# Sequence half of a two-stage kernel: decay exponents from 32-row tiles, mask in fp32r, operands and a normalising moved, new order

## The reference

```python
# block 0 (spectral): fft2 over H, W; amplitude times two sigmoid gates (C x C products); ifft2;
# 3x3 convolution; swish; plus x; layer norm over C.  The change doesn't touch it.
# block 1 (sequence): every image row of 128 positions is a sequence of length 128
u  = layernorm(z)
zg, xBC, dt = split(u @ in_proj_w.T)            # 256, 384, 8 columns
xBC = silu(causal_conv(xBC, 4 taps) + conv_b)   # x: 8 heads x 32, B: 64, C: 64
dt  = softplus(dt + dt_bias);  A = -exp(A_log)
# per head: h = h * exp(dt*A) + dt*x (outer) B;  y = h . C
y   = ssm_scan(x, dt, A, B, C) + D * x
y   = rmsnorm(y * silu(zg)) * ssm_norm_w @ out_proj_w.T
z   = z + linear_ff(y)
out = z + fc2(gelu(fc1(layernorm(z))))
```

## Time and profile before

| | |
|---|---|
| runs | 4972.34 us median of 3 (4968.33 to 4972.8) |
| profiled execution | 4973.1 us, span 4971.3 us, mean granted PE clock 0.983 |
| PE busy | 4777.4 us (96%) |
| DVE, ACT, POOL busy | 3626.1, 3136.8, 1884.9 us |
| first half (spectral) | up to about 2115 us |
| sequence half | outputs from 2220.5 us on, one per step of 21.71 us |

### The profile page before, as it was taken

One profiled execution on the slowest core, in us unless ns is written; L12 is line 12 of the kernel. 1 busy time (PEld: TensorE's weight loads), 2 busy tenths in 40 slices (PEclk: granted clock), 3 DMA queues, 4 the chain that ended last, 5 costly groups with the idle time before them and its releaser, 6 DMA issues.

```text
span 4971.3 us, 93964 instructions
## 1 busy us (share of the span) xinstructions
PE 4777.4 (96%) x31687; PEld 3555.1 (72%) x31687; DVE 3626.1 (73%) x9341; ACT 3136.8 (63%) x4388; POOL 1884.9 (38%) x2150
## 2 busy tenths in 40 slices
PE   7999999999999999969999999999999999999998
PEld 4888669875988498736766666666667666666766
DVE  4346542655166615659999999999999999999997
ACT  4211421133112411159999999999999999999997
POOL 0011000110011001135566556656655665566564
PEclk9999999999999999979999999999999999999999
DMA  2012201230023001211111111111111111111110
GB/s 78 1 50 70 85 1 35 70 100 0 20 70 99 17 5 62 68 38 37 36 36 36 36 38 36 36 36 36 36 36 38 36 36 36 36 38 36 36 36 24
DMA packets 216359, 205.38 MB, mean 41 GB/s; under 512 B 15904, under 2 KB 150688, under 8 KB 216224
## 3 DMA queue, kind: packets, MB, share of 16 engines
q1 hardware_dynamic: 216224, 203.58, 13.1%
HBM read 136.41 MB, written 67.11 MB: 41 GB/s over the span
## 4 chain that ended last, share of the span: by engine, by line
PE 30%; ACT 23%; issue 3%; DVE 0%; ACTq 0%; POOL 0%; POOLq 0%; DVEq 0%
PE g_ps L935 6%; PE g_ps L931 5%; PE g_ps L874 4%; ACT g_acc L1041 3%; ACT L1101 3%; ACT L1135 3%; PE g_ps L919 3%; ACT g_tap L1046 3%; PE g_ps L903 3%; ACT g_emat L1078 2%; PE g_ps L920 2%; PE g_ps L965 2%; ACT L1098 2%; ACT g_gl L1093 2%; ACT g_bmat L1054 2%
## 5 line engine op out<-in xcount | busy, mean ns | idle before, releaser
L1186 DVE SCALAR_TENSOR_TENSOR g_acc<-g_ps,g_conv_w,g_acc 128x504 f32<-128x504 f32 (+2 forms) x896 | 651.6, 727 | 11.6 <-ACT g_tap L1046 11.6
L1243 DVE TENSOR_TENSOR g_mmat<-g_emat,g_ps 128x1024 f32<-128x1024 f32 x512 | 616.5, 1204 | 1.5 <-PE g_ps L892 0.8
L381 ACT ACTIVATE f_conv_v<-f_ps,f_bias 128x512 f32<-128x512 f32 x128 | 87.9, 687 | 782.3 <-PE f_ps L213 782.3
L1078 ACT ACTIVATE g_emat<-g_ps 128x1024 f32<-128x1024 f32 x512 | 494.4, 1017 | 44.3 <-PE g_ps L920 44.3
L919 PE MATMUL g_ps<-g_rz,g_l 128*128 128x512 f32 x1024 | 481.6, 532 | 27.7 <-ACT g_emat L1078 25.1
L211 PE MATMUL f_ps<-f_s_hi,f_wf_hi 128*128 128x512 f32 x1152 | 468.4, 407 | 2.3 <-DVE f_s_lo L398 2.3
L213 PE MATMUL f_ps<-f_s_hi,f_wf_lo 128*128 128x512 f32 x1152 | 457.9, 397 | 0.0
L212 PE MATMUL f_ps<-f_s_lo,f_wf_hi 128*128 128x512 f32 x1152 | 457.1, 397 | 0.0
L768 POOL TENSOR_TENSOR g_sqs<-g_sq 128x256 f32<-128x256 f32 x256 | 186.7, 729 | 660.6 <-ACT g_sq L1083 660.6
L920 PE MATMUL g_ps<-g_mask_b,g_ident_b 128*128 128x512 bf16 x1024 | 400.2, 391 | 0.0
L540 POOL TENSOR_SCALAR f_rstd<-f_mv 128x4 f32<-128x4 f32 x128 | 40.9, 320 | 839.4 <-DVE f_mv L414 839.4
(11 more groups left out here) (178 smaller groups left out, 12118.7 us busy)
## 6 DMA issues: line engine op xcount, KB each, us to landing
f_xt<-in_x_cols SPq DMA_DIRECT2D x128, 256.0 KB, 2.9
f_xres<-in_x SPq DMA_DIRECT2D x128, 256.0 KB, 2.7
z<-f_zout SPq DMA_DIRECT2D x128, 256.0 KB, 2.1
g_zin<-z SPq DMA_DIRECT2D x128, 256.0 KB, 2.7
g_zres<-z SPq DMA_DIRECT2D x128, 256.0 KB, 2.7
out<-g_outb SPq DMA_DIRECT2D x128, 256.0 KB, 2.0
f_wf_raw<-in_w_f SPq DMA_DIRECT2D x1, 576.0 KB, 5.1
g_wx<-in_in_proj_t SPq DMA_DIRECT2D x1, 192.0 KB, 2.5
```

The costliest lines, as they stand in the source:

```text
L1078: act.activation(emat[:, g, :].rearrange("p (b n) -> p b n", b=2), ps[:, D_BANK[g]:D_BANK[g] + 2, :], ACT.Exp).then_inc(e_a[g], 1)
L1186: dve.scalar_tensor_tensor(out=acc[:, j, :, k:], in0=four(ps[:, bank, :])[:, :, 0:P - k], scalar=conv_w[:, j, 3 - k:4 - k], in1=acc[:, j, ...
L1243: dve.tensor_tensor(mmat[:, g, :].rearrange("p (h n) -> p h n", h=HEADS), emat[:, g, :].rearrange("p (h n) -> p h n", h=HEADS), ps[:, CB, ...
```

## The change

Only the sequence half is changed.

- `decays`: the left operand is one [128, 128] tile in place of [128, 4, 128], laid out so that 32 partitions hold everything for one group and four heads (both parts of the sums on either side). For each half of the heads there is one matmul on 32 rows (`tile_position`), the two halves on neighbouring row groups into two banks; after both, two matmuls over the full array add the mask, which is now fp32r like its identity.
- The order of (group, head) in dt, dta, dtx and in the bias and A is permuted to fit (`blocks`); dt's bias is spread once before the loop.
- The left operand comes from one ACT pass over q (`left`), and the rows for `right` from another (`right_rows`); DVE's `right` then covers 128 partitions. POOL's `left` and the two constant passes of ACT go.
- The second norm is on POOL (`norm_h`, two passes of [128, 512]), DVE's `norm` goes.
- Other PSUM banks, other `held` waits, and a new order in every `body` except SP's: cross and all four decays of a quad are now in one step, ACT has four table loads per step (Silu, exponential and logarithm, Silu, Gelu).

```diff
+def blocks(t):
+    return t.rearrange("p (a b c h) -> p a b c h", a=2, b=2, c=2)
...
-        UT, HT, F1 = 0, 2, 4
-        X_BANK, BC_BANK, Z_BANK = (5, 2), 6, (0, 5)
-        CB, XT_BANK, D_BANK, Y_BANK = 4, (3, 5), (0, 2, 0, 2), (1, 3)
-        SS, OUT, F2 = 1, 4, 4
+        UT, HT, F1 = 4, 4, 3
+        X_BANK, BC_BANK, Z_BANK = (3, 2), 5, (2, 6)
+        CB, XT_BANK, D_BANK, Y_BANK = 0, (6, 1), (2, 0, 4, 4), (1, 6)
+        SS, OUT, F2 = 5, 6, 3
...
-            def left(x):
-                pool.wait_ge(q_d, x.n + 1)
-                held(pool.wait_ge, sqs_p[0], x.n, QUADS)
-                pool.tensor_tensor(l4[64:P], q[64:P, :].bitcast(FP).unsqueeze(1).to_broadcast([64, 4, P]),
-                                   ind_g[64:P, :].unsqueeze(2).to_broadcast([64, 4, P]), ALU.mult).then_inc(l4_p, 1)
+            def norm_h(x):
+                pool.tensor_tensor(hc[:, :, :], z2[:, :, :], mv2[:, :, 0:1].to_broadcast([P, 4, P]),
+                                   ALU.subtract).then_inc(hc_p, 1)
+                pool.wait_ge(r2_p, x.n + 1)
+                pool.wait_ge(hc_p, x.n + 1)
+                pool.tensor_tensor(hn[:, :, :], hc[:, :, :], r2[:, :].unsqueeze(2).to_broadcast([P, 4, P]),
+                                   ALU.mult).then_inc(hn_p, 1)
...
             def decays(x, g):
                 pe.wait_ge(rz_d, x.n + 1)
-                pe.wait_ge(l4_p, x.n + 1)
-                if g == 0:
-                    pe.wait_ge(e_a[2], x.n + 1)
-                if g == 1:
-                    pe.wait_ge(e_a[3], x.n + 1)
+                pe.wait_ge(l4_a, x.n + 1)
                 if g == 2:
                     held(pe.wait_ge, rsv_d, x.n, QUADS)
                 if g == 3:
-                    held(pe.wait_ge, conv_d[1], x.n * 2 + 4, 2 * QUADS)
+                    pe.wait_ge(e_a[2], x.n + 1)
                 for half in range(2):
-                    dst = four(ps[:, D_BANK[g] + half, :])
-                    pe.matmul(dst, l4[:, g, :], rz[:, 4 * half:4 * half + 4, :], start=True, stop=False)
-                    mm = pe.matmul(dst, ident_b[:, :], mask_b[:, :].unsqueeze(1).to_broadcast([P, 4, P]),
-                                   start=False, stop=True)
+                    rows, first = slice(64 * (g // 2) + 32 * half, 64 * (g // 2) + 32 * half + 32), 4 * (g % 2)
+                    pe.matmul(four(ps[:, D_BANK[g] + half, :]), l4[rows, :], rz[rows, first:first + 4, :],
+                              start=True, stop=False, tile_position=(rows.start, 0))
+                for half in range(2):
+                    mm = pe.matmul(four(ps[:, D_BANK[g] + half, :]), ident_r[:, :],
+                                   mask_r[:, :].unsqueeze(1).to_broadcast([P, 4, P]), start=False, stop=True)
                 mm.then_inc(d_mm[g], 1)
...
+            def right_rows(x):
+                act.wait_ge(q_d, x.n + 1)
+                act.activation(qr[:, :], q[:, :].bitcast(FP), ACT.Identity, bias=sides[:, 1:2], scale=sides[:, 0:1]).then_inc(qr_a, 1)
+
+            def left(x):
+                act.wait_ge(q_d, x.n + 1)
+                act.activation(l4[:, :], q[:, :].bitcast(FP), ACT.Identity, bias=sides[:, 0:1], scale=sides[:, 2:3]).then_inc(l4_a, 1)
...
             def right(x):
-                dve.wait_ge(q_d, x.n + 1)
-                dve.tensor_tensor(rz[0:64], q[0:64, :].bitcast(FP).unsqueeze(1).to_broadcast([64, HEADS, P]),
-                                  p_indh[0:64, :].unsqueeze(2).to_broadcast([64, HEADS, P]), ALU.mult).then_inc(rz_d, 1)
+                dve.wait_ge(qr_a, x.n + 1)
+                dve.tensor_tensor(rz[:, :, :], qr[:, :].unsqueeze(1).to_broadcast([P, HEADS, P]),
+                                  p_indh.unsqueeze(2).to_broadcast([P, HEADS, P]), ALU.mult).then_inc(rz_d, 1)
```

More of the change, by code:

```diff
@@ L976, in body @@
                     project_bc(a_)
+                    project_z(a_, 1)
                 if b:
-                    cross(b)
-                    decays(b, 0)
-                    decays(b, 1)
-                if a_:
-                    project_z(a_, 1)
-                    project_z(a_, 0)
+                    mix(b, 0)
+                if c:
+                    turn_h(c)
                 if b:
                     mix(b, 2)
+                if c:
+                    ffn1(c)
+                if b:
                     mix(b, 3)
+                    mix(b, 1)
                 if a_:
                     cumulate(a_)
-                if b:
-                    mix(b, 0)
+                    project_z(a_, 0)
                 if p:
@@ L993, in body @@
                 if c:
[L994 removed]
+                    ffn2(c)
+                if b:
+                    project_out(b)
+                    sums(b)
+                if a_:
+                    decays(a_, 1)
+                if p:
+                    project_dt(p)
+                if a_:
+                    decays(a_, 2)
+                    decays(a_, 0)
+                    cross(a_)
+                    turn_x(a_, 0)
+                    decays(a_, 3)
+                if p:
+                    project_x(p, 0)
                 if a_:
                     turn_x(a_, 1)
[L997 to L1002 removed]
                 if p:
                     project_x(p, 1)
[L1005 to L1015 removed]
             pipeline(pe, QUADS, body)
@@ L1136, in body @@
+                    left(a_)
                     silu_c(a_)
+                    silu_b(a_)
+                    silu_x(a_, 1)
+                    act.preload_act_table_set("natural_log_exp_and_others")
+                    exps(a_, 1)
+                    exps(a_, 2)
+                    exps(a_, 0)
                 if p:
                     absolute(p)
+                    exp_dt(p)
+                if a_:
+                    exps(a_, 3)
+                if p:
+                    second_tap(p, 0)
+                    tap(p, 0)
+                    log_dt(p)
+                    second_tap(p, 1)
+                    act.preload_act_table(ACT.Silu)
+                    silu_z(p, 1)
+                    tap(p, 1)
@@ L1140, in _ @@
+                if b:
+                    affine_h(b)
+                if p:
+                    tap(p, 2)
+                if b:
+                    act.preload_act_table(ACT.Gelu)
+                    gelu(b)
             pipeline(act, QUADS, body)
@@ L1346, in body @@
                 if a_:
-                    scale_x(a_, 0)
-                if p:
-                    taps(p, 1, 2)
-                    add_bias(p)
+                    right(a_)
             pipeline(dve, QUADS, body)
```

230 lines of the change are left out of this document (86 added, 144 removed).

## The result

The changed kernel took 5061.4 us (median of 4 runs, 5056.7 to 5071.5) against 4970.4 (4 runs, 4968.3 to 4972.8): ratio 1.0186, 95% interval 1.0167 to 1.0204. It is 91 us slower. I had forecast 4982 and a range up to 5040. The profiled execution took 5065.4 us with a span of 5063.6, 92.3 more than the span before.

What follows compares the result with a forecast made beforehand. TensorE alone was taken to bound the changed kernel: 21.31 + 0.50 for four excursions = 21.81 us a step against 21.71. The profiled 4973.1 + 13 over 124 steps - 4 for ramp and drain gave 4982 us, range 4880 to 5040.

Steps and rivals of the forecast that it cites:

- ramp and drain: Before the second output and at the end: fewer wide steps, other small passes; -4 us, bounds -10 to +5.
- PE work without the tiles: 21.31: TensorE's work per step in the new order, before the 32-row tiles: 21.36 - 0.05 = 21.31 us.
- The new waits on PE are fulfilled: PE's new waits on other engines' results in the new order would be met 0.6 to 2.3 us ahead.
- the 0.36 us of waits: PE's waits per step for DVE's tap and ACT's exponentials before the change; they would go.
- Two tiles side by side: In decays(g), the two 32-row matmuls stream together: three streams instead of four, one stream being 0.21 to 0.23 us.
- One excursion into row tiles costs 0.40 us: Tiling-mode switch in each decays(g) on PE: 0.09 + 0.20 + 0.11 us; four excursions added a step.
- it can be fetched ahead: In decays(g), the mask's 128x128 weight load in fp32r could go ahead, as L919's does.
- The other engines: Busy time per step after the change: DVE about 17.7 us, POOL 14.1, ACT 19.7; only TensorE full.
- Its move costs nothing: Second normalising moved to POOL ends some 3.8 us before turn_h needs it; without that cover, up to 2.1 us a step.
- (1): Rival at decays(g) on PE: the two tiles don't overlap; 5031 us, or 5088 if streams also queue; chance 0.22.
- (2): Rival at decays(g): the mode switch costs only its drain, 0.20 us an excursion; 4883 us; chance 0.25.
- (3): Rival at ffn1: PE waits for ACT's affine of the transposed h; 4994 to 5019 us; chance 0.08.

Runs made afterwards that it cites:

- e1: Changed kernel with four left operands zero-padded to 128 rows, no 32-row tiles, ACT writing four 32-partition pieces; 5042.4 us, ratio 1.0143.
- e2: Changed kernel with dt's 8-column matmuls moved before the sums of squares, DVE's right operand reading its factor from SBUF; 5000.4 us, ratio 1.0062.
- e3: Changed kernel with one useless 512-column fp32 matmul added behind dt, its result overwritten; 5114.6 us, ratio 1.0289.
- e5: Changed kernel with the mask and its identity in bf16 instead of fp32r, nothing else; 4925.9 us, ratio 0.9908.
- e6: Changed kernel with the first decays matmul over all 128 rows of the one left operand, no 32-row tiles, result not the reference; 4914.7 us, ratio 0.9892.
- e8: e5 with decays 2 and 0 in one excursion: four 32-row tiles on four row groups, then four masks; 4859.3 us, ratio 0.9778.
- e11: e8 with the masks and their identity in fp32r instead of bf16; 4912.9 us, ratio 0.9886.
- e9: e5 with the second normalising back on DVE in four instructions instead of POOL's two passes; 4926.2 us, ratio 0.9910.

## Why the prediction was wrong

**The step that failed: the clock.** The sum took 124 steps at the granted clock of 1.00 that the earlier trace rows show and had no term for another; none of the rivals was one on the clock. Of the 83 us by which the profiled execution missed, 78 are of the clock, 12 of a longer step, and the ramp and drain took 6 back. The new order puts the tiles' switches, dt's small matmuls and the cross products one behind the other. The clock fell there 25 times, at 3.1 us each: 78 us. Take them off, and the profiled execution would be 5065.4 - 78 = 4987 us, 5 above the forecast; that it is so near is in part luck, since the other two misses offset each other. e1, e2, e3, e5, e6, e8 and e11 change that stretch in several ways and each ends the low clock. The profile of before could have told only that a full PE is no promise: in its ramp PE is busy 3.40 of 3.40 us from 2170.50 to 2173.90 at a granted clock of 0.51, though there it had just waited 1.96 us for ACT. In the changed kernel no wait stands in front.

**The sum of PE's work.** "PE work without the tiles: 21.31": e6 measured 21.35. "The new waits on PE are fulfilled": none was seen. Both right, and with them the claim that the 0.36 us of waits go.

**The tiles.** "Two tiles side by side": right. The changed kernel alone doesn't settle it, since 0.43 us from the tiles to the first mask is also what two streams of 0.215 would take in line; e8 does, with four tiles in 0.44. "One excursion into row tiles costs 0.40 us": counted as there (a full exponent 0.92, three streams 0.645), the changed kernel's 0.55 us over e6 make it 0.92 + 0.55/4 - 0.645 = 0.41. In bf16 it is 0.92 + 0.07/4 - 0.645 = 0.29. The term was right in size, with 0.014 too little on each of four exponents and 0.04 on the rest: the step became 21.91 and not 21.81, +12 us. Its parts were not: the way into row tiles costs 0.17 us behind the sums (from their start to the first exponent 0.986 against 0.813 in e6) and 0.07 behind dt (0.883 against 0.809), where I had counted 0.09 for each. What I also had wrong is whose term it is. I put fp32r on the credit side ("it can be fetched ahead"). Behind a switch it isn't: the two masks of decays 1 take 0.56 us in the changed kernel (3025.48 to 3026.04) and 0.45 in e5 (3005.14 to 3005.59), while e6, with fp32r masks and no switch, has 0.45 too. By e5 against the changed kernel the format is worth 0.49 us a step, some 61 us, and it made the thin stretch long enough to lose the clock, the other 75. One line of the change turns 0.9% faster into 1.9% slower.

**Ramp and drain**: -4 forecast; -11.5 to the first output and +1.3 behind output 126, without the low stretch of the first step. That is 6 us less than the forecast and just past the bound of -10; it makes up for half of what the longer step adds. No run takes the ramp apart.

**The other engines**, from the 124 steps: DVE 2266.2/124 = 18.3 us a step (forecast 17.7), ACT 20.2 (19.7), POOL 14.0 (14.1). ACT's two 128x128 passes are 0.49 each and not 0.35. All have room beside 21.9, so it cost nothing. "Its move costs nothing": right, by e9. But it also freed less than the 2.5 us that I took from the mean of 0.68 in the earlier trace rows: back on DVE in e9, the four pieces take 1.5 us (the last section shows where the rest was).

**The rivals.** (1), tiles that don't overlap, is false; its 5031 and 5088 lie around the measured time by chance, and the time alone would have seemed to prove it. (2), a switch that costs only its drain (0.20), is false: 0.41, and 0.29 in bf16. (3), ffn1 waiting for ACT, was not seen.

**What stays open.** Why the clock falls in 25 steps and not in all, since they are alike by their rows. It isn't random: from the first to the last, the long steps stand 2, 5 or 8 steps apart and no other distance occurs. And where exactly the limit lies: the runs show on which side of it ten versions of the new order are (the changed kernel alone on the wrong one), not more.

## What to carry to other kernels

Where TensorE sets the time, look after a reordering not only for waits but for small matmuls and switches of the tiling mode that now stand one behind the other, and read the granted clock step by step, not over the span: a PE that is 100% busy can lose it, and one more short piece of work decides. Each excursion into row tiles costs 0.3 to 0.4 us, so put as much into one as the row groups hold, and keep the weights that follow a switch in a type that loads fast. A forecast of a PE-bound loop needs a case with the low clock even if the loop before shows none.

## What the runs showed of the hardware that I had not expected

Useless matmuls of 0.96 us a step cost only 0.43 (53 us over 124 steps), because the clock stays up with them. Four 32-row tiles take the time of two (0.44 and 0.43 us to the next group). An ACT pass over 128 elements takes 0.49 us on 32 or on 128 partitions. DVE's product over 128x1024 took 2.09 us with both inputs in SBUF (e2) and 1.21 with one in PSUM (the changed kernel). The two timelines, e2 and then the changed kernel, have the same product of POOL beside it at the same time:

```profile
3022.91 1.28 POOL L810 TENSOR_TENSOR g_zresb<-g_zres,g_ffb 128x512 f32<-128x512 f32 x1
...
3023.18 2.09 DVE L1235 TENSOR_TENSOR g_rz<-g_qr,g_ind_h 128x1024 fp32r<-128x1024 f32 x1
```

```profile
3022.91 1.28 POOL L810 TENSOR_TENSOR g_zresb<-g_zres,g_ffb 128x512 f32<-128x512 f32 x1
...
3023.18 1.21 DVE L1234 TENSOR_TENSOR g_rz<-g_qr,g_ps 128x1024 fp32r<-128x1024 f32 x1
```

In e2 it starts 0.27 us behind a product of POOL, which ends 1.01 us later (3024.19), and the product is 0.88 us longer than with an input in PSUM. The Trainium skill (SBUF — State Buffer, SBUF: two separate sides) says that DVE and GpSimd lock one pair of ports in turn, and that a DVE operation with two SBUF inputs waits for the whole GpSimd one. The rows agree; no run has the two SBUF inputs without POOL beside them. The second normalising showed a wait too. Its mean of 680 ns in the earlier trace rows is of four unlike pieces: 0.74 and 1.31 us for the two that ran beside POOL's 512-column products, 0.34 and 0.33 for the two that didn't. In e9 it stood elsewhere in DVE's order, and only the first piece met the end of such a product (0.42 us, the others 0.34). These pieces have one SBUF tensor as input and not two, and I didn't test the reason.

```profile
L1288 DVE TENSOR_SCALAR g_hn<-g_z,g_mv,g_r 128x128 f32<-128x128 f32 x92 | 28.4, 368 | 0.0
```
